# Moving the absolute sum of w2 from VectorE to ScalarE in the output-projection stage of a transformer layer

## The reference

```python
x = x + attn(layernorm(x), Wq, Wk, Wv, Wo)      # 4 x 4096 x 1024, 16 heads, rotary, softmax
x = x + ffn(layernorm(x), w1, b1, w2, b2)       # 1024 -> 4096 -> 1024

def act_quant(x):
    scale = 127.0 / jnp.clip(jnp.max(jnp.abs(x), axis=-1, keepdims=True), 1e-05)
    return jnp.clip(jnp.round(x * scale), -128.0, 127.0) / scale
def weight_quant(w):
    scale = 1.0 / jnp.clip(jnp.mean(jnp.abs(w)), 1e-05)
    return jnp.clip(jnp.round(w * scale), -1.0, 1.0) / scale
def bitlinear(x, w, b):
    return einsum(act_quant(rmsnorm(x)), weight_quant(w)) + b
def ffn(x):
    return bitlinear(gelu(bitlinear(x, w1, b1)), w2, b2)
```

## Time and profile before

| quantity | value |
|---|---|
| time, median of 2 runs | 2843.54 us |
| time of the profiled execution | 2859.05 us |
| span of its slowest core (core 5) | 2857.5 us |
| spans of all eight cores | 2825.8 to 2857.5 us |
| TensorE, VectorE, ScalarE busy in the span | 2246.2, 1067.2 and 1600.6 us |

### The profile page before, as it was taken

How to read it: one execution, slowest core, us unless ns; L and a number is a source line. 1 busy time by engine, 2 the same in 40 slices (tenths; PEclk the granted TensorE clock), 3 DMA queues, 4 the chain that set the end, 5 groups by cost and what they waited for, 6 DMA issues and landing times.

```text
span 2857.5 us, 33149 instructions; the slowest of 8 cores (2825.8 to 2857.5 us)
## 1 busy us (share of the span) xinstructions
PE 2246.2 (79%) x8940; PEld 762.2 (27%) x8940; DVE 1067.2 (37%) x1941; ACT 1600.6 (56%) x2139; POOL 181.1 (6%) x345
## 2 busy tenths in 40 slices
PE   4679999888888888888888888553047988889888
PEld 1323333322222222222222222121013433334333
DVE  2434435501111111101222220188536666666664
ACT  3301101288989998889998889411414434434332
POOL 4211001000000000000000000011200000000000
PEclk8799889988989898889988889886557889888888
DMA  9632123411101111101111110376510000000000
GB/s 158 94 60 59 44 49 72 98 42 30 52 23 45 30 52 30 52 1 45 45 45 60 42 37 3 84 233 206 188 48 1 30 30 16 30 16 30 31 15 23
DMA packets 72194, 160.57 MB, mean 56 GB/s; under 512 B 8144, under 2 KB 41040, under 8 KB 70736
## 3 DMA queue, kind: packets, MB, share of 16 engines
q0 software_dynamic: 48544, 104.90, 16.0%
q1 hardware_dynamic: 23472, 53.55, 5.1%
HBM read 158.42 MB, written 29.36 MB: 66 GB/s over the span
## 4 chain that ended last, share of the span: by engine, by line
PE 42%; ACT 28%; DVE 12%; issue 10%; DMA 5%; DVEq 1%; ACTq 1%; POOL 0%; POOLq 0%; SPq 0%
ACT Et L686 24%; PE ps_b L1269 8%; PE ps_b L1317 8%; PE ps_k L405 6%; PE ps_v L380 4%; PE ps_tr L1302 3%; PE ps_cA L621 2%; PE ps_S L656 2%; DMA xb<-x_fm 2%; PE ps_cB L627 2%; DMA w2st<-w2T 2%; DVE wtmp L878 1%; PE ps_k L412 1%; DVE q1fm L1152 1%; PE ps_n L421 1%
## 5 line engine op out<-in xcount | busy, mean ns | idle before, releaser
L686 ACT ACTIVATE Et<-ps_S,negG 128x1024 bf16<-128x1024 f32 x1024 | 1046.9, 1174 | 85.8 <-PE ps_S L661 78.8
L656 PE MATMUL ps_S<-Qp,Kp 64*128 64x512 bf16 x1024 | 411.8, 407 | 120.0 <-ACT Et L686 72.4
L621 PE MATMUL ps_cA<-Et,V_sb 128*65 128x512 bf16 x1024 | 436.1, 426 | 43.5 <-DVEq L768 36.9
L661 PE MATMUL ps_S<-Qp,Kp 64*128 64x512 bf16 x1024 | 423.2, 418 | 0.0
L627 PE MATMUL ps_cB<-Et,V_sb 128*65 128x512 bf16 x1024 | 413.9, 404 | 0.0
L756 DVE COPY rlbc<-ps_rl 64x512 f32<-64x512 f32 x32 | 21.8, 683 | 772.5 <-PE ps_rl L638 772.5
L1269 PE MATMUL ps_b<-w1q,q1fm 128*128 128x512 bf16 x1024 | 256.0, 416 | 1.3 <-DVEq L1154 1.1
L656 PEld LDWEIGHTS ps_S<-Qp,Kp 64*128 64x128 bf16 x1024 | 93.6, 94 | 594.6 <-issue 594.6
L493 ACT ACTIVATE ksq<-krot 128x512 bf16<-128x512 bf16 x96 | 60.4, 630 | 321.1 <-DVEq L461 321.0
L1317 PE MATMUL ps_b<-w2q,q2fm 128*128 128x512 bf16 x1024 | 226.3, 382 | 2.0 <-DVEq L1184 2.0
L621 PEld LDWEIGHTS ps_cA<-Et,V_sb 128*65 128x65 bf16 x1024 | 113.3, 111 | 302.1 <-issue 295.5
(11 more groups left out here) (193 smaller groups left out, 2158.7 us busy)
## 6 DMA issues: line engine op xcount, KB each, us to landing
w1st_<-w1T POOLq DMA_DIRECT2D x64, 512.0 KB, 4.0
w2st<-w2T POOLq DMA_DIRECT2D x64, 512.0 KB, 4.5
xb<-x_fm POOLq DMA_DIRECT2D x64, 128.0 KB, 9.3
xr<-x_fm POOLq DMA_DIRECT2D x64, 128.0 KB, 4.8
kscr<-krot SPq DMA_DIRECT2D x64, 128.0 KB, 1.8
Kp<-kscr SPq DMA_DIRECT2D x8, 1024.0 KB, 4.9
xq<-x_tmq SPq DMA_DIRECT2D x16, 512.0 KB, 6.9
y1scr<-y1r SPq DMA_DIRECT2D x16, 512.0 KB, 6.0
```

Source lines behind the costliest of these rows:

```text
L621: e.matmul(ps2_cA[:], V_sb[:, jj * VBLK + (2 * m) * VW: jj * VBLK + (2 * m) * VW + VW], Et[itp % 4][:, 0:512], start=(jj == 0), stop=(jj = ...
L656: e.matmul(ps2_S[it % 2][:, 0:512], Kp[m % 2][0:64, j * 128:(j + 1) * 128], Qp[m % 2][0:64, qh * 512:(qh + 1) * 512], start=True, stop=Tru ...
L661: e.matmul(ps2_S[it % 2][:, 512:1024], Kp[m % 2][64:128, j * 128:(j + 1) * 128], Qp[m % 2][64:128, qh * 512:(qh + 1) * 512], start=True, s ...
L686: e.activation(Et[it % 4][:], ps2_S[it % 2][:], AF.Exp, bias=negG[:, m:m + 1], scale=1.0).then_inc(SM["aEX"], 1)
```

## The change

VectorE no longer takes the absolute sum of the w2 chunks. ScalarE does so, right behind the two squares of the same pass: two ACTIVATE instructions with function Abs for each chunk, one per half of 512 columns, whose row sums go to two columns of the small tile `scr4` (two more for the odd chunk). VectorE waits for the new semaphore `aWp` and adds the two columns to `wsum2`. `vW2` still comes from VectorE. ScalarE waits for the load of the chunk and, from chunk 2 on, for `vW2` of the chunk two before, so that the columns are free.

```diff
@@ stage 4, VectorE, in the loop over i @@
                 e.drain().then_inc(SM["vP4a"], 1)
                 for ch in (2 * i, 2 * i + 1):
-                    e.wait_ge(SM[["dW2a", "dW2b", "dW2c"][ch % 3]],
-                              16 * (ch // 3 + 1))
-                    e.reduce_sum(wtmp1[:], w2st[ch % 3][:], axis=AX,
-                                 apply_absolute_value=True)
+                    p = 2 * (ch % 2)
+                    e.wait_ge(SM["aWp"], ch + 1)
+                    e.tensor_tensor(wsum2[:], wsum2[:],
+                                    scr4[:, 8 + p:9 + p], ALU.add)
                     e.drain()
-                    e.tensor_tensor(wsum2[:], wsum2[:], wtmp1[:], ALU.add)
+                    e.tensor_tensor(wsum2[:], wsum2[:],
+                                    scr4[:, 9 + p:10 + p], ALU.add)
                     e.drain().then_inc(SM["vW2"], 1)
@@ stage 4, ScalarE, in the loop over i @@
                              accum_out=sqb_t[:, i:i + 1])
                 e.drain().then_inc(SM["aP4a"], 1)
+                for ch in (2 * i, 2 * i + 1):
+                    p = 2 * (ch % 2)
+                    e.wait_ge(SM[["dW2a", "dW2b", "dW2c"][ch % 3]],
+                              16 * (ch // 3 + 1))
+                    if ch >= 2:
+                        e.wait_ge(SM["vW2"], ch - 1)
+                    e.activation(ps3_sq[:], w2st[ch % 3][:, 0:512], AF.Abs,
+                                 accum_out=scr4[:, 8 + p:9 + p])
+                    e.drain()
+                    e.activation(ps3_sq[:], w2st[ch % 3][:, 512:1024],
+                                 AF.Abs, accum_out=scr4[:, 9 + p:10 + p])
+                    e.drain().then_inc(SM["aWp"], 1)
```

More of the change, by code:

```diff
@@ L74, in build_nc @@
             "dWO", "dWOb", "vCVo", "dXQa", "dXQb", "pY", "vY1", "dY1a", "dY1b",
-            "dW2a", "dW2b", "dW2c", "vW2", "aW2",
+            "dW2a", "dW2b", "dW2c", "vW2", "aW2", "aWp",
             "dYLa", "dYLb", "dYLc", "vP4a", "aP4a", "pIC", "vIC", "vW2q", "dB",
```

## The result

The changed kernel takes 2882.81 us (median of 11 runs), the kernel before 2843.18 us (10 runs in the same comparison). The ratio is 1.0123, with a 95% interval of 1.0099 to 1.0147: slower by 1.2%. That is less than the 2% that the prediction took as the least that can be told from no change, but the interval is narrower than that and lies clear of one. The difference of the medians is 39.6 us; the prediction's was 39.7. Medians are over all executions and ratios over the fast ones alone, because in some executions (one of the changed kernel, two of e1, one of e4, one of the kernel before beside these two) the cores of one die ran at a lower granted clock and took longer.

What follows compares the result with a forecast made beforehand. VectorE's instruction stream was taken to bound stage 4's loop; a pass of 11.55 us against 9.15 adds 38.4 us over 16 passes, plus 1.3 for the table load, giving 2883.2 us, range 2868 to 2900.

Steps and rivals of the forecast that it cites:

- handover: Stage 4's loop, each pass: from ScalarE's signal to VectorE's start, 0.13 us.
- table load: First pass of stage 4's loop: one load before ScalarE's first square, now waited for by VectorE, adds 1.29 us once.
- step 5: End of each pass in stage 4's loop: VectorE's two adds of the second chunk, 0.41 us with their gap.
- The unshown cost of Abs: ScalarE in stage 4's loop: Abs, absent from the trace, taken at the square's 602 ns, up to 630.
- The gap between pairs: ScalarE in stage 4's loop: drain, signal and up to two waits between ACTIVATE pairs, 0.23 us each, two per pass.
- The squares come onto the path too: Stage 4's loop: ScalarE's squares, hidden behind VectorE's reduces before, now delay the pass; a pair takes 1.52 us.
- The first adds cost nothing: Stage 4's loop: VectorE's adds of the first chunk, about 0.6 us, lie beside ScalarE's 1.52 us on the second.
- What stays at nothing: w2 loads, TensorE and ScalarE's new waits add nothing; the factors (8.7 us), second w2 pass (83 us) and stage 5 keep their length.
- VectorE's waits: Stage 4's loop: first small add waits about 3.5 us for ScalarE, the third about 1.2, some 75 us in total.
- A: Rival, stage 4's loop: ScalarE's work overlaps VectorE's, pass 7.06 us, 33 us less, 2810 us; 1%.
- B: Rival, stage 4's loop: ScalarE reloads its function table between Square and Abs, 40 us more, 2923 us; 4%.
- C: Rival, stage 4's loop: VectorE was already waiting, so part of the cost is hidden, under 25 us; 3%.

Runs made afterwards that it cites:

- e1: The changed kernel with ScalarE's four Abs of each pass moved ahead of its wait for VectorE's maximum; 2821.61 us, ratio 0.9889 to the kernel before.
- e4: The changed kernel with Abs ahead of the wait, w2 loads released by ScalarE, VectorE reducing 64 columns once after the loop; 2814.55 us, ratio 0.9853.
- e6: The changed kernel with a one-column ScalarE square ahead of its first wait in stage 4, so the table load runs early; 2877.99 us.
- e2: The changed kernel with ScalarE still waiting for VectorE's maximum first, then doing the four Abs, then the two squares; 2851.07 us.
- e5: e4 with w2 loads from the fourth chunk on fetching only the first 512 columns, leaving out part of the computation; 2787.74 us.

## Why the prediction was right

The prediction was 2883.2 us, 39.7 more than before; the medians say 2882.81 and 39.6. Agreement within 1 us is partly luck, since the interval of the ratio alone is 14 us wide. The loop is the better test: 38.5 us more, 1.2 us less than worked out. Its terms, against the pass shown (1838.80 to 1850.28) and ScalarE's next pass:

| step | predicted, us | measured, us |
|---|---|---|
| 1: L861 to the first square | 5.60 | 1855.88 - 1850.28 = 5.60 |
| 2 and 3: six ACTIVATE, gaps | 4.56 + 0.46 = 5.02 | 1860.85 - 1855.88 = 4.97 |
| 4: handover | 0.13 | 1860.98 - 1860.85 = 0.13 |
| 5: the two last adds | 0.41 | 1849.89 - 1849.50 = 0.39 |
| 6: gap ahead of L861 | 0.39 | 0.39 |
| the pass | 11.55 | 11.48 |
| table load, once | 1.29 | 1.30 (e6) |

(1860.98 is the start of VectorE's add behind that pair, 1860.85 the end of the accumulator read that starts at 1860.66.)

- *What bounds it*: VectorE's stream, with no slack. Right; what was added behind the maximum, 38.5 us in the loop, is in the time, 39.6 by the medians.
- *The unshown cost of Abs*: 602 ns, the value taken. *The gap between pairs*: 0.21 against 0.23. Together with step 5 that is 0.07 us a pass too much, or 1.1 in 16 passes, nearly all of the 1.2.
- *The squares come onto the path too*: right, and the largest part. e2 measures 25 us for them.
- *The first adds cost nothing*: right; they end at 1848.16, and VectorE waits 1.34 us more.
- *What stays at nothing*: the factors 8.73 against 8.72 us. TensorE's matmuls stayed off the path: no wait of VectorE for it behind the first tile. Its granted clock fell from 0.78 to 0.69 in the loop, with longer pauses between its tiles. The second pass over w2, from its first L932 to its last, 80.3 us before and 2102.5 - 2020.5 = 82.0 after; behind it, 774.4 and 773.2 us to the end of the span.
- *VectorE's waits*: 3.49 and 1.34 us, for 3.5 and 1.2 predicted; 78.7 us in total, for 75. Sixteen passes make 77.3 of it; the rest is the table load, which the 75 left out.
- *A miss*: ScalarE's squares and Abs were to make about 40% of the chain in the loop. The chain's line for the changed kernel has 30.9%:

```profile
by line: issue 11.4%; DVE ps_u L869 11.1%; DVE mx_t L872 10.6%; DVE y1r L861 10.6%; DVE s_t L864 10.5%; ACT ps_sq L959 10.4%; ACT ps_sq L956 10.4%; ACT ps_sq L947 5.2%; ACT ps_sq L944 4.9%; ACTq L961 2.4%; ACTq L958 2.1%; DVE wsum L878 1.4%
```

I had counted the accumulator reads and the gaps as ScalarE's; the view files part of them under its sequencer (ACTq) and under issue. The six ACTIVATE alone, 6 x 0.602 = 3.61 us of 11.55, are 31%. The durations were right and the share was not; shares by name are a poor thing to predict from.

The rivals. A, the overlap, did not happen, and e1 shows that it was one reordering away: in the right order seven of 15 passes take about 7.03 us, where A's working said 7.06, and the kernel is faster, 2821.61 us where A said 2810. The mean pass is 7.37 us. VectorE's waits for sums whose loads came late, which A had not priced, make some 0.28 us of the excess of 0.34, and small delays of the kind told at the end the rest. The Trainium skill's advice (Perfetto Trace Analysis, Optimizing Scalar/DVE Operations) to move work from a saturated VectorE to ScalarE therefore holds in this loop in e1 and e4, and fails in the change. B, table loads between Square and Abs, did not happen: one load in the loop. The Trainium skill (ScalarE: Activation LUTs, Table sets: the hidden batching unit) says that abs sits in every set; the trace agrees as far as it can, since it has Abs under one table only. C, hidden slack: none.

## What to carry to other kernels

Moving work to an idle engine helps only if the work is placed in that engine's stream where the engine is idle. Before counting busy shares, ask of the receiving engine: what ends its idle time, and does the one that wants the result wait right behind that? If so, the two engines take turns, and whatever already stood behind the same signal (here the squares, hidden until then) comes onto the path with it. Put work whose inputs do not depend on the signal ahead of the wait, give each result its own place so that nobody has to fetch it inside the loop, and then look at the transfers, which are the next to bind.

## What the runs showed of the hardware that I had not expected

- The loads of w2 stretch as the loop gets shorter. Median from issue to landing, with the share of the DMA engines in the loop: 3.6 us in the change (0.49), 4.5 before (0.65), 5.5 in e1 (0.78), 7.2 in e4 (0.88). I had carried 4.5 us over from the earlier trace rows to e1. The row of the change in the list of issues over its loop (KB each, us to landing):

```profile
w2st<-w2T POOLq DMA_DIRECT2D x30, 512.0 KB, 3.6
```

And the same row of e4, in a window of 102 us:

```profile
w2st<-w2T POOLq DMA_DIRECT2D x29, 512.0 KB, 7.2
```

- A high share alone does not make ScalarE wait. In e5's loop the DMA engines are busy at 0.79, as in e1 (0.78), and ScalarE waits for no load; in e1 it waits 31.9 us. Two things differ: e1's loads wait for VectorE's adds behind the maximum and e5's only for ScalarE's own sums, and most of e5's are half the size and land in 4.1 us. The runs do not separate the two.

- Now and then an instruction starts about 0.35 us late with nothing named for it, for example in e2, between two adds that are otherwise 0.24 us apart:

```profile
1854.46 0.16 DVE L878 TENSOR_TENSOR wsum<-wsum,scr 128x1 f32<-128x1 f32 x1 [1.33 <-ACTq L955]
1855.04 0.16 DVE L881 TENSOR_TENSOR wsum<-wsum,scr 128x1 f32<-128x1 f32 x1 [0.43 <-issue]
```

  It occurs in several of the kernels, the one before among them, and a loop of 16 passes is therefore up to about 1 us longer than the sum of its passes. What causes it was not tried.
